# Preparing the next block's digits in step 11 of a slot in place of step 8

## The reference

```python
for i in range(E):                                     # E = 16
    gate_feature = hidden_states * pe[i] @ gate_w + gate_b
    gate_weight, gate_idx = jax.lax.top_k(gate_feature, K)          # K = 96
    gate_weight = jax.nn.softmax(gate_weight, axis=-1)
    gathered = jnp.take_along_axis(hidden_states, gate_idx, axis=-1)
    y = y + _moe_mlp(gathered * gate_weight, eg_w[i], eu_w[i], ed_w[i])
```

## Time and profile before

| | |
|---|---|
| median of 3 runs | 2657.36 us (2656.84 to 2658.69) |
| the profiled execution, time | 2657.78 us |
| its span (first to last instruction) | 2655.9 us |
| mean granted TensorE clock | 0.905 |
| instructions | 48030 |

### The profile page before, as it was taken

The page is one execution under the profiler, slowest core; times in us unless marked ns, Lnnn a source line. Parts: engine busy times, 40 slices in busy tenths (PEclk is TensorE's granted clock), DMA queues, the critical chain, the costliest instruction groups (busy, mean ns, idle before and its releaser), DMA issues.

```text
span 2655.9 us, 48030 instructions
## 1 busy us (share of the span) xinstructions
PE 2278.8 (86%) x11466; PEld 1235.3 (47%) x11466; DVE 2513.5 (95%) x13427; ACT 1690.0 (64%) x3970; POOL 1747.4 (66%) x2109
## 2 busy tenths in 40 slices
PE   4478999989999889898999989898989888888878
PEld 3245545445454444454544545444445444443344
DVE  3699599999999999999999999999999999999993
ACT  2243677767677676676685766767766766666663
POOL 1133868667677677685785877767767677676673
PEclk9576999989898989898898999898989998989798
DMA  2202122222222221222221312122222122221211
GB/s 61 58 18 48 49 55 49 55 50 53 45 56 56 49 54 50 50 53 45 56 56 43 69 42 62 45 53 50 62 44 57 45 53 47 51 53 44 52 46 29
DMA packets 124846, 133.67 MB, mean 50 GB/s; under 512 B 39931, under 2 KB 112710, under 8 KB 124558
## 3 DMA queue, kind: packets, MB, share of 16 engines
q1 hardware_dynamic: 123140, 127.91, 20.7%
q0 software_dynamic: 880, 1.62, 0.2%
q10 hardware_dynamic: 546, 1.06, 0.1%
HBM read 102.77 MB, written 27.87 MB: 49 GB/s over the span
## 4 chain that ended last, share of the span: by engine, by line
DVE 85%; PE 7%; DMA 3%; issue 2%; ACT 1%; SPq 1%; POOL 1%; ACTq 0%; POOLq 0%
DVE idx L630 30%; DVE keys L632 29%; DVE vals L626 24%; PE ps L1232 1%; DMA rows<-digit_d 1%; DMA digit_d<-dcode 1%; DMA looked_s<-in_mask_in 1%; PE ps L1313 1%; DVE nmax L586 1%; PE ps L1286 1%; SPq L468 1%; DVE ntop L602 1%; PE ps L1220 1%; PE ps L1289 0%; DVE digits L607 0%
## 5 line engine op out<-in xcount | busy, mean ns | idle before, releaser
L1068 POOL TENSOR_TENSOR picked<-looked_s,code 128x384 f32<-128x384 f32 (+1 forms) x896 | 880.8, 991 | 498.9 <-ACT looked_s L815 497.2
L630 DVE FIND_INDEX8 idx<-vals,keys 128x8 uint16<-128x192 f32 x2712 | 940.1, 347 | 0.0
L626 DVE MAX8 vals<-keys 128x8 f32<-128x192 f32 x2712 | 820.6, 342 | 41.8 <-ACT keys L769 41.8
L815 ACT ACTIVATE looked_s<-ps 128x384 f32<-128x384 f32 (+1 forms) x896 | 440.0, 491 | 648.9 <-PE ps L1232 647.1
L632 DVE MATCH_REPLACE8 keys<-vals,keys 128x192 f32<-128x192 f32 x2486 | 840.3, 338 | 0.0
L1232 PE MATMUL ps<-code,table 128*128 128x384 f32 (+1 forms) x1824 | 839.8, 544 | 0.0
L805 ACT ACTIVATE code<-ps 128x768 f32<-128x768 f32 (+1 forms) x896 | 725.1, 809 | 57.5 <-PE ps L1220 53.5
L1220 PE MATMUL ps<-rows,codew 17*128 17x384 bf16 (+1 forms) x1824 | 320.3, 348 | 213.1 <-ACT code L805 146.3
L1220 PEld LDWEIGHTS ps<-rows,codew 17*128 17x128 bf16 x1824 | 86.8, 92 | 769.1 <-ACT code L805 400.8
L1232 PEld LDWEIGHTS ps<-code,table 128*128 128x128 f32 x1824 | 311.9, 203 | 203.9 <-issue 161.3
L1289 PE MATMUL ps<-xwt,wexp 96*96 96x128 f32 x1792 | 265.0, 294 | 35.9 <-ACT xwt L776 33.6
(11 more groups left out here) (161 smaller groups left out, 2250.7 us busy)
## 6 DMA issues: line engine op xcount, KB each, us to landing
wexp<-in_w_exp SPq DMA_DIRECT2D x58, 576.0 KB, 4.4
wdown<-in_w_down SPq DMA_DIRECT2D x58, 576.0 KB, 4.5
digit_d<-dcode SPq DMA_DIRECT2D x56, 384.0 KB, 2.6
rows<-digit_d SPq DMA_DIRECT2D x224, 96.0 KB
table<-norm_d SPq DMA_DIRECT2D x448, 3.0 KB
patch<-in_patches SPq DMA_DIRECT2D x16, 108.0 KB, 4.9
tok_d<-h SPq DMA_DIRECT2D x16, 84.8 KB
norm_d<-hs SPq DMA_DIRECT2D x16, 84.8 KB
```

Of the source, the lines that this page charges most:

```text
L626: nc.vector.max(vals[:, par, e, at], from_keys[:, e, :]).then_inc(chain, 1)
L630: found = nc.vector.max_index(idx[:, par, e, at], vals[:, par, e, at], from_keys[:, e, :])
L815: nc.scalar.activation(looked_s[:, o % 4, 0:w], ps[:, LOOK_B[o % 2], 0:w], ACT.Copy).then_inc(looked_out, 1)
L1068: nc.gpsimd.tensor_tensor(picked[:, o % PICKS, w], looked_s[:, o % 4, w], code[:, o % 4, 1, w], ALU.mult).then_inc(picked_ready, 1)
```

## The change

One number changes. It moves three things in every slot from the first to the one before the last: the digits copy from step 8 to step 11 on ACT, the four exponentials from steps 9 to 12 to steps 12 to 15 on ACT, and the squares from step 8 to step 11 on POOL.

```diff
-PREPARE = 8
+PREPARE = 11
```

## The result

The changed kernel takes 2970.01 us in the median, against 2657.1 us before: a ratio of 1.1169, 95% interval 1.1132 to 1.1205. The forecast was 2930 us, with a range of 2795 to 3040. A fourth execution of the changed kernel took 4953.37 us, at a granted clock of 1.00; no run shows why, and it is not counted. The profiled execution took 2972.36 us, its span 2970.5 us, with a mean granted clock of 0.849 (0.905 before).

The account below looks back on a forecast made before the run. DVE was taken to bound the kernel from 312 us, the change handing the bound to the loop through SyncE, PE, ACT and POOL. 215 + 16 + 27 + 15 = +273 us on 2657.8 gave 2930 us, range 2795 to 3040.

Parts of the forecast that it names:

- The bound: Over the kernel from 312 to 2585 us: DVE's rankings alone set the time, 43.6 us a block with attention.
- the trip: Digits' copy, square, store and load until PE's first code: 12.5 us, with only 5.5 us of cover from step 11.
- 43 blocks with attention: Blocks while attention runs: period rises from DVE's 43.6 to 48.6 us, +215 us.
- 10 blocks after it: Last ten blocks, no attention left: period rises from 42.6 to 44.2 us, +16 us.
- extra for the clock, 53 x 0.5: PE behind its new stall in each block: slower clock costs 0.5 us a block, +27 us.
- start, up to block 3: Before 312 us: digits of blocks 1, 2 and 3 come three steps later, 5 us each, +15 us.
- tail from the last first code: From the last block's first code to the end: unchanged at 58.9 us.
- The steps: Step 14 of one slot to step 11 of the next: thirteen at 2.6 us, 33.8 us.
- A: Steps 11 to 14 cover the digits' way after all, DVE keeps the bound: about 2670 us, chance 0.05.
- B: ACT's 118.4 us of waits for DVE vanish and the start is pulled in: 2630 us, chance 0.02.
- C: Every PE stall is followed by a slow-clock stretch costing 5.7 us a block: 3100 us, chance 0.06.
- Nothing for them: Exponentials moved to steps 12 to 15 on ACT: they fit before POOL's read in the next slot, no cost.

Follow-up runs that it names:

- The fills: Changed kernel plus matmuls nobody reads in PE's stall before each block's first code: six took 2956.04 us, thirteen 2896.44 us.

## Why the prediction was right

**The bound** was read rightly: before, DVE is hardly ever idle from 312 to 2585 us; after, it is out of the chain. **The mechanism** is the trip that had six steps of cover and has three. Moving only the digits gives all of the loss, moving only the exponentials at most 8 us, and a us off the trip is a us off the period.

**The terms of the sum**, as the prediction put them and as measured:

```text
term                                   predicted          measured
43 blocks with attention               +215 (48.6 us)     +274.9 (49.98 us)
10 blocks after it                     + 16 (44.2 us)     + 23.7 (44.92 us)
extra for the clock, 53 x 0.5          + 27               in the two lines above
start, up to block 3                   + 15               + 16.5
tail from the last first code          0                  - 0.5
sum                                    +273               +314.6
```

The 42 us that are missing come from *the trip*. It was put at 12.5 us, from three blocks of the kernel before, and is 13.46 on average: 1.0 us on 53 blocks is 51 us, and the other terms together take some 10 back. Some 0.7 us of it is a queue that I looked up in the order of POOL and did not price: the squares' new place stands behind a unit's products, and they start 1.88 us behind the copy, where in the three blocks they started 1.75, 0.92 and 0.92 behind it, 1.20 in the mean. The block at 1.75 is block 46, whose trip of 13.56 was the longest of the three: the sign of the queue stood in the rows. Another 0.2 us lie between the issue of the last load and the code (6.21 against 5.97). The prediction says of a step that is moved only what it waits for; what stands ahead of it in its new place counts as well.

*The steps* were put at 33.8 us plus 0.5 for the clock and take 34.18. That this fits is luck, for two errors cancel. The pace of 2.6 us is a mean over all sixteen steps. The first ten took 25.11 us in the kernel before, and the three from look 8 to look 11 take 6.52 in the changed one, 31.6 together: 2.2 us under the 33.8, and next to the 31.5 of slot 29 that I set aside as no average. The clock's term was too small by about as much: the first ten steps grew to 27.66 us, 2.55 more, where 0.5 was put. My reason for the low value, that the old stalls would vanish and that they cost the same, did not hold: inside these ten steps slow clock had stood in 19 of 43 slots, and behind the new stall it stands in all 43.

*The start* came out near its +15, but by the other runs' spread there (303 to 314 us for block 3) this too is no close test.

**The rivals.** A (cover after all) and B (faster) are ruled out: PE waits in 57 of 57 blocks. (By the prediction's own lag and trip, A needs steps of 4.9 us and not 4.5: three of them less 2.3 us against 12.5.) C (the full price of the clock, 3100 us) was right in kind and wrong in size: every stall is followed by slow clock, as that rival said (in 43 of 43 slots), but it costs 2.7 us a block and not 5.7. The 5.7 us came from two stretches that do not hold the same work: 56 matmuls in slot 21 and 38 in slot 23. Of the 56, these 24 have no like in slot 23:

```profile
1111.68 4.61 PE L1179 MATMUL ps<-v,probt 113*113 113x17 f32 x24
```

In slot 29 the stretch behind the stall shows what each part is like, in windows of the changed kernel (columns as in the earlier trace rows); 1.2 GHz for most of the first 13.6 us, full clock in the 12.8 us that follow:

```profile
1666.40:1680.00 13.60, 13.57 (x60) 8.24 (x61) 11.25 (x63) 6.57 (x16) 4.17 (x5) 0.62 0.28 75
1680.00:1692.80 12.80, 11.50 (x71) 8.14 (x70) 12.80 (x72) 9.74 (x25) 10.68 (x15) 1.00 0.18 46
```

The Trainium skill ("TensorE: Matmul & The Clock Gate", the section on the HAM clock gate) has it that the default is half rate and that activity lifts it. The fills agree: with six matmuls and idle time left behind them slow clock follows in 38 of 43 slots, with thirteen and almost none left (0.1 us in the mean) in 15.

**Signs.** Of those named in advance: DVE's share 85% (86% said), waits for keys 15 times (every fourth block), for digits down to 1.9 us, PE's wait for `rows` 424.7 us in 57 blocks (250 or more), though of the waits of blocks 4 to 56 only 31 of 53 are 4 to 8 us long, as I had said, and 19 are longer, up to 9.7, DMAs in the chain 18% (both of digits and rows), periods of 50.0 and 44.9 us (47 to 50 and 44 to 46), a lower clock. Not named: DVE's 48.5 us for exponentials. "Nothing for them" held for the time, not for the waits. The nothing put for SyncE's other transfers held too: behind the start, the only DMA that PE is seen to wait for is that of `rows`.

## What to carry to other kernels

A hand-over through DRAM has a length that hardly depends on where it begins (here copy, squares, store, loads: 13.0 to 13.6 us in the mean when PE had to wait for it and POOL made the squares, 11.7 with the squares on ACT), and the steps between its start and its use are its cover. Add up just those steps, one by one, for they are not alike (1.0 to 4.1 us here, each a mean over 43 slots); subtract how late the issuing engine runs; and compare. As long as the cover holds, shortening the trip gives nothing; once it doesn't, each us counts in each round, and here stalls of PE of 5.3 and 7.0 us in the mean cost another 2.7 to 3.0 us through its clock. A kernel bound by one engine can hide a second ring that is within 2 us of it, so look at the pace of every ring without its waits before moving a start later. When two stretches are compared for the price of a clock, count their instructions first.

## What the runs showed of the hardware that was not expected

The price of the clock is no line in the length of the stall. Over the 25.11 us of the kernel before (0.8 us idle before the first code), the same ten steps took 0.9 us more with 1.6 us of idle time, 2.6 more with 5.3, and 2.55 more with 7.0 (two other runs with the copy in step 8 took 25.00 and 25.51 us, so 0.9 us is little above the spread); slow clock was 6.0, 6.7, 12.1 and 13.6 us a block. Nor is all time at slow clock paid for: in the changed kernel 3.8 of the 13.6 us fall into the stall, and inside the steps 6.8 us less of it (8.9 to 2.1) gave 2.7 us. Half a fill does not help half: 4.03 us of matmuls in front of 4.89 us of idle time gave 14 us, 8.55 us without idle time behind them 74 us, in spite of an overrun. And the fill is no repair: at step 11 it leaves 239 us of the loss, of which the overrun is some 70 (43 x 1.7) and the rest the trip that isn't covered.
